# Edge attention in a four-layer graph network: one-hots stored once and read back, masks folded into the matmul that spreads the scores, relu in place of leaky relu

## What is computed

```python
xl = (h @ Wl + bl).reshape(N, H, HD)          # H = 4 heads of HD = 32
xr = (h @ Wr + br).reshape(N, H, HD)
e = leaky_relu(xl[src] + xr[dst], 0.2)
score = einsum('ehd,hd->eh', e, att)
m = segment_max(score, dst)
ex = exp(score - m[dst])
den = segment_sum(ex, dst)
out = segment_sum((ex / den[dst])[:, :, None] * xl[src], dst)
```

## Time and profile before

| | us |
|---|---|
| median of 3 runs | 8590.22 (8582.79 to 8591.82) |
| the profiled execution, its own time | 8583.67 |
| its span, first to last instruction | 8581.6 |
| PE busy in the span | 5951.0 (69%) |
| DVE busy | 5586.0 (65%) |
| POOL busy | 3924.9 (46%) |
| ACT busy | 3686.5 (43%) |
| `mlp_pass`, about | 3419 to 4623 |
| `gatv2_pass`, first and second, about | 4795 to 6400, 6474 to 8086 |

### The profile page before, as it was taken

How to read it: one execution, slowest core, us unless ns; L and a number is a source line. 1 busy time by engine, 2 the same in 40 slices (tenths; PEclk the granted TensorE clock), 3 DMA queues, 4 the chain that set the end, 5 groups by cost and what they waited for, 6 DMA issues and landing times. The chain is left out here.

```text
span 8581.6 us, 178520 instructions
## 1 busy us (share of the span) xinstructions
PE 5951.0 (69%) x52869; PEld 5066.3 (59%) x53419; DVE 5586.0 (65%) x16634; ACT 3686.5 (43%) x8315; POOL 3924.9 (46%) x3723
## 2 busy tenths in 40 slices
PE   2222227666586775999997588888866888888577
PEld 2222214555476774777775477777755777777577
DVE  8444426987586685444444688888876887787712
ACT  1111101677575573444444355555544554454400
POOL 2777731788300000777772455555525555555200
PEclk9999998876698997999998799999988999999788
DMA  4111140233242241233334111111131111111355
GB/s 168 53 53 52 52 162 17 95 110 113 94 154 98 95 154 59 76 76 72 73 72 28 37 38 37 39 37 38 37 24 41 38 36 36 37 37 37 21 194 200
DMA packets 472947, 619.50 MB, mean 72 GB/s; under 512 B 283561, under 2 KB 381654, under 8 KB 453588
## 3 DMA queue, kind: packets, MB, share of 16 engines
q1 hardware_dynamic: 362948, 414.53, 14.6%
q0 software_dynamic: 109568, 200.53, 10.8%
HBM read 468.42 MB, written 146.37 MB: 72 GB/s over the span
## 5 line engine op out<-in xcount | busy, mean ns | idle before, releaser
L980 POOL DMA_INDIRECT rows<-source_table,idxb x2640 | 2526.2, 957 | 2899.1 <-ACT idxb L1000 1154.8
L1607 DVE CUSTOM_DVE_ANT_0 junk<-pen,ps_top 128x512 f32<-128x512 f32 x1760 | 1135.8, 682 | 140.5 <-PE ps_top L1763 133.8
L360 POOL DMA_INDIRECT records<-recb,idxb x784 | 762.8, 973 | 256.0 <-issue 247.1
L774 PE MATMUL ps_cells<-hot 128*128 128x128 bf16 x4608 | 529.6, 263 | 307.2 <-ACT ps_cells L793 174.2
L1763 PE MATMUL ps_top<-srow,sel 128*128 128x128 bf16 x7040 | 628.3, 225 | 130.8 <-ACT srow L1667 86.8
L1087 PE MATMUL ps_acc<-rows,pt 128*128 128x128 f32 x3750 | 516.3, 280 | 134.9 <-DVE pt L1108 120.3
L774 PEld LDWEIGHTS ps_cells<-hot 128*128 128x128 bf16 x4608 | 398.0, 120 | 358.6 <-issue 345.6
L388 PE MATMUL ps_g<-hott 64*128 64x128 bf16 x784 | 101.0, 308 | 718.8 <-ACT hott L404 714.7
L1763 PEld LDWEIGHTS ps_top<-srow,sel 128*128 128x128 bf16 x7040 | 451.9, 105 | 237.2 <-issue 155.3
L1726 PEld LDWEIGHTS ps_e<-ident,rows 128*128 128x128 f32 x3520 | 535.2, 218 | 82.0 <-issue 24.3
L1087 PEld LDWEIGHTS ps_acc<-rows,pt 128*128 128x128 f32 x3750 | 461.3, 192 | 168.5 <-DVE pt L1108 161.2
(11 more groups left out here) (311 smaller groups left out, 15060.3 us busy)
## 6 DMA issues: line engine op xcount, KB each, us to landing
logs<-log_counts SPq DMA_DIRECT2D x75, 1600.0 KB
wt<-edge_weights SPq DMA_DIRECT2D x50, 1600.0 KB
rows<-source_table,idxb POOLq DMA_INDIRECT x2640
edge_weights<-both SPq DMA_DIRECT2D x125, 320.0 KB, 2.8
log_counts<-none SPq DMA_DIRECT2D x125, 320.0 KB, 2.2
records<-blank SPq DMA_DIRECT2D x16, 1870.0 KB
feat<-records SPq DMA_DIRECT2D x220, 128.0 KB, 2.3
rb<-records SPq DMA_DIRECT2D x6, 4352.0 KB
```

Source lines behind the costliest of these rows:

```text
L360: g.indirect_dma_start(out=recs[:, :], out_offset=bass.IndirectOffsetOnAxis(ap=idxb[k][:, t:t + 1], axis=0), in_=recb[k][:, t, :], in_offs ...
L774: pe.matmul(tile[:, 0:P], hot[k][:, 0, j // 2, :, j % 2], hot[k][:, m, j // 2, :, j % 2], start=False, stop=m == 4, skip_group_check=True)
L980: g.indirect_dma_start(out=rows[r][:, k, :], out_offset=None, in_=table, in_offset=bass.IndirectOffsetOnAxis(ap=idxb[r][:, k:k + 1], axis= ...
L1607: ve.tensor_tensor_reduce(out=junk[h % 2][:, :], in0=pen[mk][:, :], in1=ps_top[h % 2][:, :], scale=1.0, scalar=-BIG, op0=ALU.add, op1=ALU.max,
```

## The change

Five things at once, and what they bring with them:

1. `mlp_pass` stores `hot` (fp32, 128x512) and `hott` (bf16, 128x512) of every group to DRAM (SP, two DMAs a group); `gatv2_pass` loads both back per group (SP) and makes neither. Its `hott` has four buffers in place of two.
2. The mask goes into the spreading product: rows 64 to 127 of `parts` hold 16 digit indicators of each edge's target (`c.digits`, copied per group by ACT) and `c.sel` holds -2^100 where a node's digit does not match. `mask_tables` builds both, once. DVE takes plain maxima of `ps_top` in PSUM (`tensor_reduce`), from three PSUM buffers in place of two.
3. Leaky relu is 0.2 x plus 0.8 relu(x): ACT takes a relu of `ps_e`, `att` is scaled by 0.8, and the linear part (0.2 x score of the source row) comes with the gathered row, as 4 more columns of the table; 4 columns of ones give the denominator. A row of the table is 136 floats (544 B) in place of 128. The target's linear part cancels in the softmax.
4. DVE evicts the scores from PSUM, adding the linear part; the running maximum is kept as `last + reset` in `sc` (no `c.top`); the exponentials of weights and of the drop are one ACT operation on 20 columns; clip, copy of the weights and two copies of maxima are gone.
5. The gathered rows enter `ps_e` and `ps_1` by PE's transposing mode (`is_transpose=True`). Order and depth: 6 stages, 13 block registers a turn.

Cut to its core:

```diff
@@ mlp_pass: SP, PE, DVE, ACT
+                    def store(i, r):
+                        n = RING * i + r
...
+                        sp.wait_ge(hot_ready, n + 1)
+                        sp.dma_start(hots[:, at, :]..., hot[r]...).then_inc(hot_stored[r], 16)
+                        sp.wait_ge(hott_ready, n + 1)
+                        sp.dma_start(hotts[:, at, :]..., hott[r % 4][:, :]).then_inc(hott_stored[r % 4], 16)
...
-                                ins = pe.matmul(ps_1[mk][...], rows[r][:, q, :], c.ident[:, :], start=False, ...)
+                                                is_transpose=True, start=False, stop=q == TG - 1)
...
+                            wait(ve, hot_stored[r], 16 * i)
                             one_hot(ve, c, hot[r], fg).then_inc(hot_ready, 1)
...
-                            wait(act, sum1, g - 1)
+                            wait(act, sum1, g - 3)
+                            wait(act, hott_stored[r % 4], 16 * (2 * i + r // 4))
@@ gatv2_pass: DVE, one step
+                        sums, weights, merge, maxima, score, _ = stages
                         if sums:
                             ve.wait_ge(rows_in[r], (i + 1) * (16 * TG))
                             ve.wait_ge(p_ready, g + 1)
+                            ve.tensor_tensor(val[k][:, :, :, :], rows[r][:, :, 0:HEADS * HW]..., p[k][:, 0:SC]..., ALU.mult)
+                            ve.tensor_tensor(faded[:, :, :], c.acc[...], p[k][:, SC:CUT]..., ALU.mult)
                         if weights:
                             ve.tensor_reduce(there...)
+                            ve.tensor_tensor(t[wr % 4][:, 0:SC], sc[wr][:, 0:SC], there[:, :], ALU.subtract)
-                            ve.tensor_scalar(t[:, :], t[:, :], 0.0, None, ALU.min)
-                            ve.tensor_tensor(lr[:, :], low[:, :], ps_e[:, :], ALU.max)
+                            ve.wait_ge(sc_ready, sg + 1)
+                            ve.tensor_tensor(sc[sr][:, 0:SC]..., ps_sc[:, 0:SC]..., rows[sr][:, :, HEADS * HW:TW], ALU.add)
+                        def top(h):
+                            ve.wait_ge(tops, HEADS * mg + (h + 1))
+                            ve.tensor_reduce(gtop[:, h:h + 1], ps_top[h % TOPS][:, :], AX.X, ALU.max)
+                        top(0)
+                            ve.tensor_copy(hi, sc[cr][:, :])
+                            ve.tensor_tensor(res[:, :], sc[cr][:, :], hi, ALU.subtract)
+                        top(1)
+                            ve.tensor_copy(mid, res[:, :])
+                            ve.tensor_tensor(lo, res[:, :], mid, ALU.subtract)
+                        top(2)
                             ve.tensor_tensor(c.acc[...], faded..., ps_acc..., ALU.add)
+                        top(3)
+                            ve.scalar_tensor_tensor(new, last, reset, gtop[:, :], ALU.add, ALU.max)
+                            ve.scalar_tensor_tensor(t[mr % 4][:, SC:CUT], last, reset, new, ALU.add, ALU.subtract)
@@ gatv2_pass: ACT, one step
+                            act.activation(srow[:, :], ps_srow[:, 0:P], ACT.Copy)
+                            act.activation(parts[score[1] % 2][:, 64:P], c.digits[...], ACT.Copy)
+                            act.activation(p[k][:, :], t[r % 4][:, :], ACT.Exp)
+                            wait(act, sc_ready, eg - 1)
+                            act.activation(bent[er % 2][:, :], ps_e[:, :], ACT.Relu)
                             next_idx(...)
@@ gatv2_pass: PE, one step, in this order
+                        transpose of parts; maxima back to edges (hott);
+                        wait bent_ready; ps_sc from bent and att4;
+                        heads 0, 1, 2 of ps_top; wait val_ready; ps_acc from hot and val;
+                        head 3 of ps_top (its buffer is that of head 0);
+                        wait hots_in, bent_ready; ps_e from c.mine and hott;
+                        wait rows_in; rows[r][:, q, 0:D] transposed into ps_e
@@ gatv2_pass: SP
+                        wait(sp, agg_done, n - RING + 1)
+                        sp.dma_start(hott[r][:, :], hotts[:, at, :]...)
+                        sp.dma_start(hot[r]..., hots[:, at, :]...)
@@ gnn_kernel, before each round of GATv2
+            mask_tables(nc, c)                       # once
+                    vector_steps(nc, turn)           # five 128x128 copies: features interleaved by head
+                        step(ve.tensor_tensor(c.other[:, :, :], rows2[:, :, D:2 * D], attr..., ALU.mult))
+                        step(ve.tensor_reduce(den[:, :, :], c.other..., AX.X, ALU.add))
+                        step(ve.tensor_scalar(linear_part, den[:, :, :], 0.2, None, ALU.mult))
+                        step(ve.memset(linear_part[64:P, NB - 1, :], -BIG))
+                    load_rows(nc, [(head_tab..., rows2[:, :, D:D + TW])])
```

More of the change, by code:

```diff
@@ L1302, in mlp_pass @@
         dist = sb("dist", [BN, GE])
-        hott = [sb(f"hott{k}", [BN, GE], BF16) for k in range(2)]
+        hott = [sb(f"hott{k}", [BN, GE], BF16) for k in range(4)]
         featt = [sb(f"featt{k}", [EF, GE]) for k in range(2)]
@@ L1478, in gatv2_pass @@
+def gatv2_pass(nc, c, table, att, hots, hotts):
+    TOPS = 3
     with ExitStack() as ctx:
@@ L1481, in gatv2_pass @@
         CUT = SC + HEADS
-        rows = [sb(f"rows{r}", [P, TG, D]) for r in range(RING)]
+        rows = [sb(f"rows{r}", [P, TG, TW]) for r in range(RING)]
         idxb = [sb(f"idxb{r}", [P, TG], I32) for r in range(RING)]
@@ L1558, in step @@
                     def step(stages):
-                        sums, weights, maxima, score, masks = stages
+                        sums, weights, merge, maxima, score, _ = stages
                         if sums:
@@ L1623, in step @@
                         if maxima:
+                            top(3)
+                            ve.wait_ge(topped, HEADS * mg + HEADS)
+                            ve.scalar_tensor_tensor(new, last, reset, gtop[:, :], ALU.add, ALU.max).then_inc(newtop, 1)
                             ve.wait_ge(newtop, mg + 1)
-                        if score or maxima:
-                            cr = sr if score else newr
-                            n = sg if score else mg + 1
-                            ck = cr % 2
-                            wait(ve, srow_ready, n - 1)
-                            wait(ve, at_edges, n - 2)
-                            hi, mid, lo = (parts[ck][:, m * CUT:(m + 1) * CUT] for m in range(PARTS))
-                            ve.tensor_copy(hi, sc[cr][:, :]).then_inc(hi_out, 1)
@@ L1642, in step @@
-                        if score or maxima:
-                            ve.wait_ge(res_ready, n + 1)
-                            ve.tensor_copy(mid, res[:, :]).then_inc(mid_out, 1)
-                            ve.wait_ge(mid_out, n + 1)
-                            ve.tensor_tensor(lo, res[:, :], mid, ALU.subtract).then_inc(lo_out, 1)
-                    pipeline(nc, ve, c, 5, step)
+                            wait(ve, p_ready, mg - 3)
+                            ve.scalar_tensor_tensor(t[mr % 4][:, SC:CUT], last, reset, new, ALU.add, ALU.subtract).then_inc(drop_ready, 1)
@@ new lines, in step @@
+                        if maxima:
+                            mi, mr, _ = maxima
+                            mg = RING * mi + mr
+                            pe.wait_ge(lo_out, mg + 1)
+                            pe.wait_ge(dig_out, mg + 1)
+                            wait(pe, srow_out, mg)
+                            pe.transpose(ps_srow[:, 0:P], parts[mr % 2][:, :], c.identb[:, :]).then_inc(srow_ready, 1)
+                        if weights:
+                            i, r, _ = weights
+                            g = RING * i + r
+                            pe.wait_ge(lo_out, g + 3)
+                            wait(pe, summed, g)
+                            maxima_parts = parts[r % 2][0:BN, 0:PARTS * CUT].rearrange("p (m j) -> p m j", m=PARTS)[:, :, SC:CUT]
+                            for q in range(TG):
+                                ins = pe.matmul(ps_node[:, q * PARTS * HEADS:(q + 1) * PARTS * HEADS]
+                                                .rearrange("p (m h) -> p m h", m=PARTS),
+                                                hott[r][:, q * P:(q + 1) * P], maxima_parts, start=True, stop=True)
+                            ins.then_inc(at_edges, 1)
@@ new lines, in step @@
+                        if score:
+                            si, sr, _ = score
+                            sg = RING * si + sr
+                            pe.wait_ge(bent_ready, sg + 1)
+                            wait(pe, sc_out, sg)
+                            for q in range(TG):
+                                ins = pe.matmul(ps_sc[:, q * HEADS:(q + 1) * HEADS], bent[sr % 2][:, q * P:(q + 1) * P],
+                                                att4[:, :], start=True, stop=True)
+                            ins.then_inc(sc_ready, 1)
@@ new lines, in spread_scores @@
```

(20 more changed lines are left out.)

440 lines of the change are left out of this document (228 added, 212 removed).

## The result

The changed kernel takes 8140.15 us (median of 4 runs, 8108.95 to 8154.23) against 8590.33 before: ratio 0.9473 [0.9445, 0.9501], 450 us less. The forecast was 8130, so total and sign were right. The profiled run took 8141.56 us, its span is 8139.8.

The account below looks back on a forecast made before the run. VectorE was taken to bound the GATv2 step and TensorE the edge MLP. Rounds -437, MLP -65 and one-time work +45 gave -457 us, so 8133 for the median, told as 8130; range 7950 to 8320.

Parts of the forecast that it names:

- VectorE's step, 5.15: GATv2 rounds: VectorE's step falls from 6.24 to 5.16 us, say 5.15, with a maximum's pitch at 0.61.
- TensorE's step, 4.8, covered: GATv2 rounds: TensorE's step is 4.5 plus some 0.3 us uncovered relu wait, 4.8, under VectorE's 5.15.
- The 2.84 us of fetching stay: VectorE's branch in the GATv2 rounds: the 2.84 us instruction fetch pause remains each turn; the branch costs 6.3 us.
- Fetch gone: Rival, VectorE's branch: the shorter list fits what the fetch holds, 52 x 2.84 = 148 us less, 7985; chance 0.14.
- The loss behind the branch, 2.0: GATv2 turns: TensorE at 1.2 GHz behind the branch costs 2.0 us a turn in place of 1.4.
- MLP, -65: MLP stage: POOL takes over as bound, 40.8 us a turn; 65 of 70 us gained after the stores' cost.
- a landing of a few us is far inside four groups: MLP stage: waits of VectorE and ACT on the new stores, eight and four groups back, are covered.
- Set-up, +45: Work added once: mask tables 24, two rounds 32, less 12, MLP's last stores 3; sum +47, rounded to +45 us.
- twelve of a quarter at 0.53 or more: `mask_tables` on POOL: twelve quarter-size selects at 0.53 us or more each, within about 20 us for POOL.
- Steps outside the turns: GATv2 rounds: 12 steps per round outside its 26 turns, each 1.1 us less, 13 us a round.
- coupling: Rival: TensorE's relu wait or POOL's 1.25 grows a tenth, step 5.5, 154 us more, 8285; chance 0.25 with slow maxima.
- half clock: Rival, steady steps of both rounds: TensorE at 1.2 GHz, step 9.3 us, 924 us more, 9500; chance 0.04.

Follow-up runs that it names:

- e9: Changed kernel plus idle semaphore increments per VectorE step (8 in round 1, 15 in round 2) and fp32 products replacing the MLP's transposes; 8597.57 us, 1.0006 of before.
- e2: Changed kernel plus two idle semaphore increments per VectorE step of the edge attention, 265 instructions a turn instead of 249; 9463.27 us, 0.9467 of before.
- e10: Changed kernel plus idle fp32 products of 256 columns on TensorE ahead of the branch, 8 in round 1, 3 in round 2; 8091.65 us, 0.9419 of before.
- e1: Changed kernel with empty slots of the edge records naming 55 rows instead of one; 9455.57 us, 0.9456 of before.
- e5: Changed kernel with empty slots naming 55 rows, mask table made for one head and copied, registers loaded only for blocks in use; 9364.71 us, 0.9365 of before.

## Why the prediction was right, and where it was not

- **VectorE's step, 5.15.** Right: 5.19 in the row above, 0.61 for a maximum. e9 shows that VectorE sets it, on chips like that of the result.
- **TensorE's step, 4.8, covered.** Right: 4.75 us where it catches up, 5.2 where VectorE holds it. The relu is uncovered by 0.53 to 0.63 us rather than 0.3. POOL did not bind the rounds.
- **The branch, "The 2.84 us of fetching stay".** This step failed, by 2.8 x 50 = 140 us. I had estimated over 250 instructions; there were 249, and what matters is a limit that lies below the 313 of e9 and above 249, or 265 with e2. The rival *Fetch gone* described it rightly and got 0.14; I took it that today's list, which does pause, shows that little is held. The Trainium skill ("Runtime: NRT & Kernel Launch", Instruction fetch mechanics) says that two blocks of 256 instructions are held and that a taken branch out of them stalls. I read that as "any list under 512 is free", and e9 speaks against this reading: 313 and 369 pause. The rule itself can stand, since a list of over 256 can touch three blocks if it begins inside one; where these lists begin is in no row, so this is argued only.
- **The loss behind the branch, 2.0.** 47.7 - 8 x 5.22 - 3.5 = 2.4. It is an alternation, 46.3 and 49.3, with a granted clock of 0.76 and 0.56 behind the branch; e10 shows that TensorE's idle time at the branch makes it. The step of 5.22 (mean of a turn's steady ones) costs 8 x 0.07 = 0.6 more. So of the 140 about 50 went back: rounds -488 in 50 turns against 50 x 7.9 = -395.
- **MLP, -65.** The mechanism was right: POOL takes over and issues without a pause; e9 gives the 0.46 a step. Common turns are 40.2 us, for POOL needs the 40.0 of its gathers and hardly any of the 0.8 added for its waits. By these turns the stage would have won 85. It won 16: the last turn costs 46 us more and a few others 2 to 6. The step that failed is "a landing of a few us is far inside four groups". The stores share the DMA engines with gathers of one repeated row, slow before the change too, when nothing waited behind them. That the repeated row slows the gathers is shown (e1); that it makes all of the 46 us on the quicker chips is argued, and the 24 us of e9 show that its price depends on the rest of the step.
- **Set-up, +45.** Too low: from the MLP's last sum to the first gather of round 1 it is 63 us more (4622.5 to 4803.0 before, 4610.5 to 4854.0 after), which the forecast itself called a sign of being wrong above 60, and between the rounds 9 more: 72 against 35 (the 45 less 10 for the sixth stage's steps). The POOL stage takes 54.3 us, where the forecast had 20 for POOL and counted the 24 of VectorE: 30 of the 37 that were missing. The term at fault is "twelve of a quarter at 0.53 or more": 3.43 each, 41.2 - 6.4 = 35 us more. I had scaled by elements; e5 shows that a quarter of the elements still leaves 23.7 of 41.2.
- **Steps outside the turns.** The forecast has a gain of 32 us in them (2 x 218 - 50 x 7.9, less those 10). The starts and ends of both rounds together are 16 us shorter; why not more was not looked into.
- **Sum.** -457 forecast, -442 measured on the span. Against the forecast: the fetch pause -140, step and loss behind the branch +47, the MLP +49, set-up +37, steps outside the turns +16, the rest +7: 16 in all. Had the pause stayed, as forecast, the rest would have put the time 155 us above the forecast; that these meet is luck.

Rivals: coupling did not come (on these chips); half clock came behind the branches alone, not in the steady steps. On the slower chips VectorE is not the bound, so the forecast's main argument fails there, yet kernels with the whole change stand at nearly the same ratio (e2: 0.9467). Why is open: the kernel before was not profiled there.

## What to carry to other kernels

Count what an engine issues in one turn of its loop, waits and register work included: at 249 and 265 the branch was free, at 313 it cost 2.9 us a turn. Load at a branch only the registers that are used, and give TensorE products to run meanwhile; on the quicker chip three (1.35 us) did nothing where eight (3.5 us, longer than the loads) took 1.5 us off a turn, and on a slower one five showed nothing. Before a loop gets its first wait on a store, look at what else is on the queues in its worst turn, padding included.

## What the runs showed that I had not expected

- Gathers of one repeated 512-byte row: 0.8 us a packet in the mean of a stretch, 0.12 for 55 rows side by side (both with the packets of 4 bytes).
- TensorE took 16 passes of idle products ahead of 3.1 us of register loads and ran them while it loaded.
- Affine selects on GpSimd cost by more than their elements: 128x512 in 3.43 us in the mean (4.5 with an inner run of one element, 1.0 with one of 32), 128x128 in 1.97, 128x2048 in 2.1.
- Idle semaphore increments stood 0.093 us apart on VectorE, the first ones beside a maximum of 512 columns, so that 8 left a gap of 0.29 us and 15 one of 0.94 (e9).
- Chips differ: on some, results of TensorE were taken up 0.8 us or more late, mostly 1.0 or 2.6, in 124 of 183 relus, and the kernel before is 16 to 18% slower.
